# Projecting the context keys for two batches at a time in a Perceiver layer

## The reference

```python
x = x + _L0_xattn_ref(_layernorm(x), ctx_1024, ctx_1024, Wq, bq, Wk, bk, Wv, bv, Wo, bo)
#   k = split_heads(key @ Wk.T + bk)            128 x 257 x 256
#   v = split_heads(value @ Wv.T + bv)
#   scores = einsum('bhnd,bhmd->bhnm', q, k);  attn = softmax(scores);  out = einsum(attn, v) @ Wo.T + bo
x = x + _L0_attn_ref(_layernorm(x), ...)        # sigmoid attention, 32 x 32, rotary
x = x + _L0_ffn_ref(_layernorm(x), ...)         # probs = softmax(tokens @ gate_w); argmax, capacity 160
```

## Time and profile before

| what | us |
|---|---|
| median of 3 runs (lowest, highest) | 1346.71 (1345.29, 1346.93) |
| the profiled execution | 1344.86 |
| its span, first to last instruction | 1343.0 |
| busy: PE, PEld | 1157.5 (86%), 936.5 (70%) |
| busy: DVE, ACT, POOL | 945.0 (70%), 872.4 (65%), 569.7 (42%) |
| mean granted TensorE clock | 0.970 |

### The profile page before, as it was taken

The page is one execution under the profiler, slowest core; times in us unless marked ns, Lnnn a source line. Parts: engine busy times, 40 slices in busy tenths (PEclk is TensorE's granted clock), DMA queues, the critical chain, the costliest instruction groups (busy, mean ns, idle before and its releaser), DMA issues.

```text
span 1343.0 us, 37302 instructions
## 1 busy us (share of the span) xinstructions
PE 1157.5 (86%) x14033; PEld 936.5 (70%) x14033; DVE 945.0 (70%) x2523; ACT 872.4 (65%) x2443; POOL 569.7 (42%) x1045
## 2 busy tenths in 40 slices
PE   6898889888888898889888888988898888864797
PEld 5676777767767777777767767767777677742697
DVE  3667777777777777777777777877777777763121
ACT  3676767777777667767777777667677777632131
POOL 1244454455444444444454444444444554431121
PEclk9899999999999999999999999999999999975899
DMA  6414211111211111111111111111111111000474
GB/s 148 126 47 144 84 57 43 51 54 51 52 40 45 49 52 47 50 47 39 46 48 50 49 30 50 49 49 46 50 40 39 48 48 45 14 9 13 115 225 153
DMA packets 71904, 81.93 MB, mean 61 GB/s; under 512 B 16987, under 2 KB 50732, under 8 KB 71728
## 3 DMA queue, kind: packets, MB, share of 16 engines
q1 hardware_dynamic: 65280, 75.19, 19.3%
q0 software_dynamic: 3200, 3.71, 0.8%
q10 hardware_dynamic: 3248, 0.66, 0.2%
HBM read 64.79 MB, written 16.56 MB: 61 GB/s over the span
## 4 chain that ended last, share of the span: by engine, by line
DVE 33%; PE 31%; ACT 20%; issue 9%; POOL 6%; SPq 0%; DVEq 0%; DMA 0%; ACTq 0%; POOLq 0%
ACT prob L739 8%; ACT wbd L799 4%; PE score L444 4%; PE vps L411 4%; PE kps L401 4%; DVE prob L974 4%; ACT qz L728 3%; DVE nmx L963 3%; PE shared L477 3%; PE shared L532 3%; PE shared L523 3%; PE score L670 3%; PE score L684 3%; DVE pr L1116 3%; POOL ctx_p L1273 2%
## 5 line engine op out<-in xcount | busy, mean ns | idle before, releaser
L739 ACT ACTIVATE prob<-score,nmx 128x257 f32<-128x257 f32 x512 | 236.2, 476 | 175.8 <-DVE nmx L963 175.0
L401 PE MATMUL kps<-ctx_p,wk_p 128*128 128x256 f32 x1536 | 213.6, 289 | 0.2 <-POOL ctx_p L1273 0.2
L411 PE MATMUL vps<-wv_p,ctx_p 128*128 128x256 f32 x1536 | 212.7, 288 | 0.0
L1273 POOL TENSOR_TENSOR ctx_p<-ctxT,ctx_p 128x512 fp32r<-128x512 f32 x128 | 152.1, 1188 | 119.8 <-ACT ctx_p L755 119.8
L411 PEld LDWEIGHTS vps<-wv_p,ctx_p 128*128 128x128 f32 x1536 | 192.6, 192 | 12.4 <-issue 12.4
L401 PEld LDWEIGHTS kps<-ctx_p,wk_p 128*128 128x128 f32 x1536 | 195.4, 192 | 5.4 <-issue 2.3
L963 DVE TENSOR_REDUCE nmx<-score 128x2 f32<-128x514 f32 x256 | 163.1, 679 | 15.7 <-PE score L428 15.7
L1291 POOL TENSOR_TENSOR plast<-const,prob 128x128 f32<-128x128 f32 x128 | 64.1, 501 | 257.7 <-DVE prob L974 257.7
L974 DVE TENSOR_SCALAR prob<-prob,rsum 128x257 f32<-128x257 f32 x512 | 158.3, 352 | 9.0
L444 PE MATMUL score<-const,prob 128*128 128x128 f32 x1024 | 145.7, 280 | 7.5 <-DVE prob L974 3.5
L444 PEld LDWEIGHTS score<-const,prob 128*128 128x128 f32 x1024 | 114.1, 142 | 44.4 <-DVE prob L974 28.6
(11 more groups left out here) (163 smaller groups left out, 2188.4 us busy)
## 6 DMA issues: line engine op xcount, KB each, us to landing
ctxT<-in_ctxT SPq DMA_DIRECT2D x128, 257.0 KB, 3.0
w<-in_w SPq DMA_DIRECT2D x16, 1024.0 KB, 9.7
xq<-in_x SPq DMA_DIRECT2D x32, 128.0 KB, 3.3
xr<-in_x SPq DMA_DIRECT2D x32, 128.0 KB, 2.5
qbd<-qkT SPq DMA_DIRECT2D x256, 16.0 KB, 1.8
out<-row SPq DMA_DIRECT2D x32, 128.0 KB, 1.9
slots<-row SPq DMA_DIRECT2D x10, 257.0 KB, 5.6
x_a<-slots SPq DMA_DIRECT2D x8, 129.0 KB, 2.1
```

Of the source, the lines that this page charges most:

```text
L401: last = mm(kps[:, c, :], wk_p[:, x, n, c * P:(c + 1) * P], ctx_p[:, g, y, n, :], start=(n, x) == (0, LO), stop=(n, y) == (C - 1, LO))
L411: last = mm(vps[:, c, :], ctx_p[:, g, x, n, c * P:(c + 1) * P], wv_p[:, y, n, :], start=(n, x) == (0, LO), stop=(n, y) == (C - 1, LO))
L739: last = af(prob[:, m, :], score[:, m, 0:S], ACT.Exp, bias=nmx[:, m:m + 1], scale=1.0, accum_out=esum[:, m:m + 1])
L1273: g.tensor_tensor(ctx_p[:, g_, LO, :, :], ctxT[:, r, :, g_, 0:SM], ctx_p[:, g_, HI, :, :].bitcast(F32), ALU.subtract).then_inc(s["ctx_part ...
```

## The change

The context parts are made for a pair of batches: `context_hi` and `context_lo` run twice a tile (slots 1 and 3) on 4 x 256 columns instead of four times on 2 x 256. The keys of a pair are projected one feature chunk c a slot: six matmuls of 512 columns (two batches side by side) in place of twelve of 256, into one PSUM bank `kps`, which ACT copies out in one instruction of 512 columns. `kT` and `ctx_p` grow to two pairs. Values stay as they were, one batch a slot. `last_key` becomes `last_keys`, a pair at a time. Loads of the context wait for the parts of a pair. In slot 3 `context_hi` now stands ahead of `probsT`; before, it stood behind it.

```diff
-        ctx_p = sb("ctx_p", [P, 2, 2, C, SM], F32R)
+        ctx_p = sb("ctx_p", [P, 2, 2, C, 2, SM], F32R)
-        kT = sb("kT", [P, 2, C, S])
+        kT = sb("kT", [P, 2, C, 2, S])
-        kps, vps = ps("kps", [P, C, SM]), ps("vps", [P, C, D])
+        kps, vps = ps("kps", [P, 2, SM]), ps("vps", [P, C, D])
...
-            def keys(t, j):
+            def keys(t, r, c):
...
-                pe.wait_ge(s["ctx_parts"], b + 1)
-                pe.wait_ge(s["k_evac"], b)
-                for c in range(C):
-                    for n in range(C):
-                        for x, y in PASSES:
-                            last = mm(kps[:, c, :], wk_p[:, x, n, c * P:(c + 1) * P], ctx_p[:, g, y, n, :],
+                pe.wait_ge(s["ctx_parts"], 2 * t + r + 1)
+                pe.wait_ge(s["k_evac"], 4 * t + 2 * r + c)
+                for n in range(C):
+                    for x, y in PASSES:
+                        last = mm(kps[:, :, :], wk_p[:, x, n, c * P:(c + 1) * P], ctx_p[:, r, y, n, :, :],
...
-            keys(0, 0)
+            for c in range(C):
+                keys(0, 0, c)
             values(0, 0)
...
-                    if ahead:
-                        keys(ta, ja)
+                    if xa and (j < 2 or q):
+                        keys(i + j // 2, 1 - j // 2, j % 2)
...
-                for c in range(C):
-                    last = af(kT[:, j % 2, c, 0:SM], kps[:, c, :], ACT.Identity, bias=b_k[:, c:c + 1], scale=1.0)
+                af(kT[:, r, c, :, 0:SM], kps[:, :, :], ACT.Identity, bias=b_k[:, c:c + 1], scale=1.0).then_inc(s["k_evac"], 1)
...
-                af(ctx_p[:, g, HI, :, :], ctxT[:, r, :, g, 0:SM], ACT.Copy).then_inc(s["ctx_hi"], 1)
+                af(ctx_p[:, r, HI, :, :, :], ctxT[:, r, :, :, 0:SM], ACT.Copy).then_inc(s["ctx_hi"], 1)
...
-                    if xa and j < 3 and (j < 2 or q):
-                        context_hi(*((i, j + 2) if j < 2 else (i + 1, j - 2)))
+                    if q and j % 2:
+                        context_hi(i + 1, j // 2)
...
-                    if xa and j == 3 and q:
-                        context_hi(i + 1, 1)
...
-                    if xa and (j < 2 or q):
-                        context_lo(*((i, j + 2) if j < 2 else (i + 1, j - 2)))
+                    if q and j % 2:
+                        context_lo(i + 1, j // 2)
```

More of the change, by code:

```diff
@@ L245, in load_ctx @@
             def load_ctx(t, r):
-                sp.wait_ge(s["ctx_parts"], floor0(TB * t + 2 * r - 2))
+                sp.wait_ge(s["ctx_parts"], floor0(2 * t + r - 1))
                 b = TB * t + 2 * r
@@ L429, in scores @@
                                   qz[rows, half, e, j, :, :].rearrange("p h q -> p (h q)"),
-                                  kT[rows, b_slot(j), e, :], start=True, stop=True)
+                                  kT[rows, j // 2, e, j % 2, :], start=True, stop=True)
                         if e and m % 2:
@@ L741, in exps, with keys, context_hi @@
                     last.then_inc(s["exp_done"], 1)
-            def keys(t, j):
-                b = TB * t + j
-                act.wait_ge(s["k_done"], b + 1)
-                act.wait_ge(s["s_done"], floor0(2 * (b - 1)))
-                for c in range(C):
-                    last = af(kT[:, j % 2, c, 0:SM], kps[:, c, :], ACT.Identity, bias=b_k[:, c:c + 1], scale=1.0)
-                last.then_inc(s["k_evac"], 1)
-            def context_hi(t, j):
-                b, r, g = TB * t + j, j // 2, j % 2
+            def keys(t, r, c):
+                act.wait_ge(s["k_done"], 4 * t + 2 * r + c + 1)
+                act.wait_ge(s["s_done"], floor0(2 * (TB * (t - 1) + 2 * r + 2)))
+                af(kT[:, r, c, :, 0:SM], kps[:, :, :], ACT.Identity, bias=b_k[:, c:c + 1], scale=1.0).then_inc(s["k_evac"], 1)
+            def context_hi(t, r):
                 act.wait_ge(ctx_in[r], 16 * C * (t + 1))
-                act.wait_ge(s["v_done"], floor0(b - 1))
-                af(ctx_p[:, g, HI, :, :], ctxT[:, r, :, g, 0:SM], ACT.Copy).then_inc(s["ctx_hi"], 1)
+                act.wait_ge(s["v_done"], floor0(TB * (t - 1) + 2 * r + 2))
+                af(ctx_p[:, r, HI, :, :, :], ctxT[:, r, :, :, 0:SM], ACT.Copy).then_inc(s["ctx_hi"], 1)
             def values(t, j):
@@ L821, in _ @@
             last.then_inc(s["klast_done"], 1)
+            keys(0, 0, 0)
             context_hi(0, 1)
-            keys(0, 0)
+            keys(0, 0, 1)
             values(0, 0)
@@ L1263, in power, with last_keys, context_lo @@
                 g.tensor_tensor(rstd[n][:, :], ve[n][:, :], k["mhalf"], ALU.pow).then_inc(s[done], 1)
-            def last_key(t, j):
-                b = TB * t + j
-                pool.wait_ge(s["s_done"], floor0(2 * (b - 1)))
-                g.tensor_copy(kT[:, j % 2, :, SM:S], klast[:, :, bass.ds(b, 1)]).then_inc(s["klast_cp"], 1)
-            def context_lo(t, j):
-                b, r, g_ = TB * t + j, j // 2, j % 2
-                pool.wait_ge(s["ctx_hi"], b + 1)
-                g.tensor_tensor(ctx_p[:, g_, LO, :, :], ctxT[:, r, :, g_, 0:SM], ctx_p[:, g_, HI, :, :].bitcast(F32),
+            def last_keys(t, r):
+                b = TB * t + 2 * r
+                pool.wait_ge(s["s_done"], floor0(2 * (TB * (t - 1) + 2 * r + 2)))
+                g.tensor_copy(kT[:, r, :, :, SM], klast[:, :, b:b + 2]).then_inc(s["klast_cp"], 1)
+            def context_lo(t, r):
+                pool.wait_ge(s["ctx_hi"], 2 * t + r + 1)
+                g.tensor_tensor(ctx_p[:, r, LO, :, :, :], ctxT[:, r, :, :, 0:SM], ctx_p[:, r, HI, :, :, :].bitcast(F32),
                                 ALU.subtract).then_inc(s["ctx_parts"], 1)
@@ L1357, in _ @@
             pool.wait_ge(s["klast_done"], 1)
-            last_key(0, 0)
+            last_keys(0, 0)
             def body(i, half):
@@ L1363, in body @@
                 for j in range(TB):
-                    if xa and (j < TB - 1 or q):
-                        last_key(*((i, j + 1) if j < TB - 1 else (i + 1, 0)))
+                    if xa and j % 2 and (j < 2 or q):
+                        last_keys(i + j // 2, 1 - j // 2)
                     if j == 0 and once(i):
```

9 lines of the change are left out of this document (4 added, 5 removed).

## The result

The changed kernel takes 1380.88 us (median of 4 runs, 1380.29 to 1382.09) beside 1346.15 us for the kernel before (4 runs). The ratio is 1.0259, with a 95% interval of 1.0242 to 1.0277. The forecast was 1372.5 us with a range of 1361 to 1388: the direction and the mechanism hold, the size is 8 us short. The profiled execution took 1380.96 us (span 1379.1), 36.1 us more than that of before.

A forecast was written before the change was run, and what follows sets the result against it. It took the tile as one chain passing between engines, with DVE's `pr` held by POOL's subtraction. 29 x 0.85 = 24.7 us plus 1.4 for the start, 26.1 on 1346.71, gave 1372.5 us, range 1361 to 1388.

The forecast's parts named there:

- The mechanism: End of slot 3: POOL's doubled subtraction holds DVE's `pr` until it ends, 0.85 us later in each of 29 tiles.
- The either-order argument: End of slot 3: if `pr` gets the port first, `eqr` is held instead and ends 0.73 us later, nearly the same.
- Keys on PE, 0: Key matmuls in every slot: six of 512 columns take as long as twelve of 256, so PE gains nothing.
- Copy of the keys on ACT, 0: One 512-column copy saves 0.26 us a slot, but ahead of copies that wait anyway; taken as 0.
- The late `probT` in slot 3, hidden: Next slot 0's scores start 0.6 to 0.7 us late, covered by waiting for DVE's maxima: 0; uncovered, 0.65 us a tile.
- The start, 1.4 us: Start of the run: one more group of six matmuls ahead of the first values costs 1.4 us.
- uncovered it would be 0.16 us: Slot 1: the wider high part delays `probT` by 0.16 us, covered by self-attention; taken as 0, otherwise 0.16 us a tile.
- The last tile, 0: Slot 2 of the last tile has one group of keys less: taken as 0, at most 1.4 us saved.
- A (DVE first): Slot 3: DVE finishes before POOL takes the port, 1321 us; 6% together with the case of ACT's and PE's savings counting.
- B: Slot 3: hold ends before POOL's instruction, or 1024 columns take hardly longer; only the start is lost, 1348 us; 5%.
- C, the late scores uncovered: Slot 0: the late `probT` is not covered and adds 0.65 us a tile, 21 us in all: 1393 us; 9%.

The follow-up runs named there:

- Experiments 2: The kernel before, with only the 512-column high part of slot 3 moved ahead of `probT`: 1329.71 us, 0.9891 of before.
- experiments 5: The kernel before, with the fourth batch's high part in slot 2 and low part early in slot 3, POOL waiting for the normalised row: 1315.45 us.
- experiment 7: The changed kernel, with POOL's 1024-column subtraction of slot 3 cut into two of 512 columns: 1366.65 us, 1.0163 of before.
- experiment 1: The changed kernel, with the high part of slot 3 put back behind `probT`: 1377.41 us, 1.0246 of before.
- experiment 3: The changed kernel, with the keys of a slot again as twelve matmuls of 256 columns: 1381.53 us, 1.0273 of before.
- experiment 9: The kernel of experiment 8, with the high part of slot 1 moved behind that slot's `probT`: 1324.99 us, 0.9852 of before.
- experiment 4: The changed kernel, with the second pair's high part made in slot 2 and its low part at the start of slot 3: 1408.4 us.
- Experiment 6: The changed kernel, with six extra 256-column matmuls behind the keys of slot 0, their output overwritten by the values: 1377.49 us, 1.0239 of before.
- experiments 8: The kernel of experiment 4, with POOL's early low part first waiting for the normalised row: 1321.12 us, 0.9821 of before.

## Why the prediction was right, and where it was short

**The mechanism is the predicted one.** The step that `pr` is held until POOL's subtraction ends, and so pays for its columns, holds in all its parts: L1266 took 2.17 us (2.10 worked out), `pr` has a median of 2.07, and the tile grew by 0.86 us (0.85 worked out). The term 29 x 0.85 = 24.7 us came out as 24.7 us in the tiles. The sum was 10.0 us short of the profiled execution (26.1 of 36.1 us); it is the start, the clock and the end that were missing. Experiments 2, 5 and 7 show it from three sides: a shorter hold, none, and two short ones, each with the tile following the hold within 0.03 us. The either-order argument was also right: with `eqr` held instead (experiment 1) the tile is within 0.05 us. It was right on when the hold ends and left open who gets the port (below). That the total came within the range owes something to the range: it was drawn for the length of the hold, and the 8 us of the miss come from elsewhere.

**Keys on PE, 0.** Right: experiment 3. Six matmuls of 512 columns take what twelve of 256 took (1.64 and 1.68 us).

**Copy of the keys on ACT, 0.** Right for the path. The saving itself was too large: a copy took 700 ns, not 600, so 0.16 us a slot and not 0.26 were there to be hidden. The copy of the keys adds a bias, which the row I went by (L770) does not. At 256 columns a copy with the bias took 489 ns (L748, kernel before) and one without 385; at 512 it is 700 and 600. The same 0.10 us at both widths points to the bias and not to the width or to the gaps in the destination; no run tried it.

**The late `probT` in slot 3, hidden.** Right, by the rows of the result, and experiment 1 agrees. I worked out scores 0.6 to 0.7 us late, and slot 3 is 0.64 us longer. In slot 1 it is hidden in a steady tile, but not in tile 1.

**The start, 1.4 us: the step that failed most.** It was 5.4 us by the end of tile 1. I counted one more group of matmuls, and not that there is a single PSUM buffer for it: the second chunk waits 0.87 us for ACT's copy of the first, and the first scores wait for `last_keys` behind POOL's wide subtraction; 2.3 us together. The first scores lie at 21.7 to 22.8 us in the profiles of the three kernels with one batch at a time, and at 24.4 to 25.5 in the eight with pairs: 2.7 us apart in the mean. The other 3.0 us are in tile 1. The largest part that has a cause in the rows is a hold that the sum left out: it counted the subtraction of slot 3 only where the gate runs, in 29 tiles, and in tile 0 it holds L951 instead (1.16 us in slot 0 of tile 1). For the wider high part the prediction had a term, "uncovered it would be 0.16 us", from steady tiles, where self-attention covers it; in tile 1 that work is not there yet. Slot 1 is 0.26 us longer than before, and experiment 9 shows that with the other order it is 0.96 us shorter. The 1.55 us of slot 2 go with a granted clock of 0.82 instead of 1.00; whether the wait of PE ahead of it brought the fall stays open, since experiments 3 and 4 have the wait and not the fall.

**The clock, no term at all.** Four tiles lost 4.3 us. I had costed waits on PE at nothing since PE idles there anyway, but in the changed kernel the clock fell to its lower level in slot 0 of these tiles. Experiment 6 fills PE's idle time and nothing else, and gains 3.4 us. In experiment 1 they are gone as well, with a longer wait in another place. So idle time of PE has a part in it; the rule by which the clock falls stays open.

**The last tile, 0.** It was +1.4 us with what follows. 0.74 us of that are in its slot 2, where the granted clock is 0.91 instead of 1.00, so they too go with the clock and not with a cost of the change's work; 0.6 us lie between the start of its last slot and the end of the run, a stretch that takes from 161.8 to 164.7 us in the profiles of this study (163.0 before, 163.6 changed).

**The rivals.** A (DVE first) fell: `pr` and `eqr` never both got through ahead of POOL. But its point was real: experiments 5 and 8 are that case brought about, and faster by 2.2% and 1.8%. B fell by the 2.07 us. C, the late scores uncovered, fell: 0.65 us a tile on top are not there.

The Trainium skill, SBUF — State Buffer, "Who interferes with whom", has the one who starts first keep the pair of ports. For the length of the hold the trace agrees: each held operation ends behind POOL's instruction, the 8 columns of `pr` and `eqr` by 0.02 to 0.03 us, the 256 of experiment 4 by 0.15 and the 512 of L951 by 0.55. For who keeps it experiment 4 does not: DVE's recorded start is 659.31, POOL's 659.37, it is so in all 29 tiles, and it is DVE that is held. In the kernel before there is the opposite case, at the start of tile 1: POOL's subtraction is recorded at 53.41 and DVE's split at 53.43, and it is POOL that takes 1.74 us instead of 1.18. The measurement decides: starts within 0.1 us of each other do not tell here who is held.

## What to carry to other kernels

When a tiny operation ends with a long neighbour on another engine, tile after tile, suspect that it is not working but held. Its price is then what is left of the neighbour's instruction: split that one, or place it where the other engine runs nothing that is held, and look at every line it lands beside, in the first tiles too. Merging instructions on GpSimd to save issue overhead can cost more on VectorE than it saves. Cost an edit at nothing only for the tiles in which its cover exists: work out the first and the last apart, and count what a longer idle time of TensorE does to its clock.
